# Split parts of x read in place as matmul weights, gathered windows placed by a table, b2 added after the last block

## The reference

```python
msg = node_feat[src] + edge_feat
neigh = jax.ops.segment_sum(msg, dst, num_segments=3125)
rst = (1.0 + eps[0]) * node_feat + neigh
h = rst @ W1 + b1                      # 128 -> 256
h = relu((h - mean(h, 0)) * rsqrt(var(h, 0) + 1e-5) * gamma + beta)
out = h @ W2 + b2                      # 256 -> 128
x = layernorm(x + out)                 # over the 128 features
```

## Time and profile before

| | |
|---|---|
| median of 3 runs | 280.7 us (280.33 to 281.25) |
| the profiled execution, its own time | 281.48 us |
| its span, first to last instruction | 279.7 us |
| mean granted TensorE clock | 0.964 of full speed |
| busy in the span | PE 244.9, DVE 208.4, POOL 181.2, ACT 131.7 us |

### The profile page before, as it was taken

One profiled execution on the slowest core, in us unless ns is written; L12 is line 12 of the kernel. 1 busy time (PEld: TensorE's weight loads), 2 busy tenths in 40 slices (PEclk: granted clock), 3 DMA queues, 4 the chain that ended last, 5 costly groups with the idle time before them and its releaser, 6 DMA issues.

```text
span 279.7 us, 7102 instructions
## 1 busy us (share of the span) xinstructions
PE 244.9 (88%) x2211; PEld 200.6 (72%) x2211; DVE 208.4 (75%) x916; ACT 131.7 (47%) x236; POOL 181.2 (65%) x117
## 2 busy tenths in 40 slices
PE   1567989999998889988899999999999859999970
PEld 1456768899987677766788888777878648844870
DVE  3888997788998778778489887876867861178990
ACT  0327864455555535545255544444443302086494
POOL 2078888888888888888888888888888920000000
PEclk9999999999999999999599999999999968999995
DMA  5955766687888777788488888776665200000033
GB/s 165 285 172 108 147 145 137 156 191 197 189 195 185 178 164 171 181 179 183 96 172 192 174 195 171 167 179 145 150 126 105 53 2 0 2 0 1 2 114 116
DMA packets 49535, 38.39 MB, mean 137 GB/s; under 512 B 5083, under 2 KB 48523, under 8 KB 49497
## 3 DMA queue, kind: packets, MB, share of 16 engines
q1 hardware_dynamic: 32829, 30.62, 38.2%
q0 software_dynamic: 14976, 6.82, 20.4%
q10 hardware_dynamic: 1692, 0.48, 0.9%
HBM read 36.31 MB, written 1.60 MB: 136 GB/s over the span
## 4 chain that ended last, share of the span: by engine, by line
PE 46%; DMA 16%; issue 14%; POOL 9%; DVE 7%; ACT 4%; SPq 2%; DVEq 0%; ACTq 0%; POOLq 0%
PE ps L641 18%; PE ps L649 12%; DMA egat<-in_x_dram,srci 9%; POOL egat L402 9%; DMA egat<-in_edge_attr_dram 7%; PE ps L679 5%; PE ps L673 4%; PE ps L595 4%; ACT big L527 3%; PE ps L665 2%; SPq L321 1%; DVE big L1033 1%; DVE big L1035 1%; PE ps L670 1%; DVE hit_l L904 1%
## 5 line engine op out<-in xcount | busy, mean ns | idle before, releaser
L402 POOL DMA_INDIRECT egat<-in_x_dram,srci x104 | 172.2, 1656 | 44.0 <-issue 29.2
L488 ACT ACTIVATE big<-ps 128x500 f32 x156 | 95.1, 610 | 119.8 <-PE ps L679 91.6
L641 PE MATMUL ps<-big,xp 128*128 128x114 f16 (+8 forms) x675 | 116.9, 280 | 0.2 <-issue 0.2
L649 PEld LDWEIGHTS ps<-hit_c,ebuf 128*128 128x128 f32 x624 | 101.8, 194 | 16.6 <-DVE aggT L983 6.1
L649 PE MATMUL ps<-hit_c,ebuf 128*128 128x20 f32 x624 | 95.1, 230 | 9.1 <-DVE aggT L983 5.0
L641 PEld LDWEIGHTS ps<-big,xp 128*128 128x128 bf16 x675 | 63.0, 110 | 14.6 <-issue 1.1
L983 DVE TENSOR_TENSOR aggT<-aggT,ps 128x20 f32 x208 | 35.8, 172 | 49.8 <-PE ps L649 39.7
L910 DVE TENSOR_TENSOR hit_k<-iota_k,key 128x400 f16<-128x400 f16 x156 | 56.1, 359 | 0.0
L904 DVE TENSOR_TENSOR hit_l<-iota_k,lo 128x256 f16<-128x256 f16 x156 | 52.1, 334 | 1.7 <-issue 1.6
L679 PE MATMUL ps<-hit_k,hit_l 128*128 128x400 f16 x156 | 52.3, 335 | 0.0
L908 DVE TENSOR_TENSOR hit_k<-iota_k,key 128x300 f16<-128x300 f16 x156 | 48.2, 309 | 0.0
(11 more groups left out here) (101 smaller groups left out, 165.5 us busy)
## 6 DMA issues: line engine op xcount, KB each, us to landing
ebuf<-in_edge_attr_dram SPq DMA_DIRECT2D x78, 256.0 KB
egat<-in_edge_attr_dram SPq DMA_DIRECT2D x51, 128.0 KB
egat<-in_x_dram,srci POOLq DMA_INDIRECT x104
out_dram<-big SPq DMA_DIRECT2D x6, 256.0 KB
w_sb<-in_L_gnn_W_dram ACTq DMA_DIRECT2D x2, 128.0 KB, 6.8
rows<-in_dst_dram SPq DMA_DIRECT2D x1, 192.0 KB
rows<-in_src_dram ACTq DMA_DIRECT2D x1, 192.0 KB
egat<-in_edge_attr_dram SPq DMA_DIRECT2D x1, 66.0 KB
```

The costliest lines, as they stand in the source:

```text
L402: return nc.gpsimd.indirect_dma_start(to, None, x[:, :], bass.IndirectOffsetOnAxis(ap=ix, axis=0), compute_op=op)
L488: nc.scalar.activation(cnt[:, :, bass.ds(lows[m % LOADS], WIN)], ps[:, m % BANKS_C, 0:KEYS].rearrange("p (t n) -> p t n", n=WIN), ACT.Copy ...
L641: last = nc.tensor.matmul(ps[:, ACC + f % 2, 0:SIZES[f]], xp[:, t, n, :], cnt[:, t, STARTS[f]:STARTS[f] + SIZES[f]], start=(u == 0), stop= ...
L649: last = nc.tensor.matmul(ps[:, SUMS + w % BANKS_S, 0:WIN], rows_v[:, j * D:(j + 1) * D], hits_v, start=(j == 0), stop=(j == ROWS - 1))
```

## The change

Three edits:

1. `xp` goes. `xr` gets room for all 25 tiles, part 2 gets a tensor of its own (`x3`), and the matmuls of parts 0 and 1 take as weights the upper halves of the fp32 words of `xN` and `xr` directly, that is every second bf16. ACT's fourteen copies and their semaphores go, and so do the waits of `rest` on them.
2. Which windows are gathered is decided by `arrange`, in the program's construction: it adds up costs in cycles window by window, and makes a window gathered when the running sum reaches GATHER_FIRST + n * GATHER. The last window stays gathered.
3. As b2's addition changes `xN`, which is now read by the matmuls, POOL waits with it for the last block's matmuls.

```diff
+ROUNDS = 12
+SUM = 670
+COUNT = 770
+KEPT = 810
+HITS = 2400
+TURN = 1680
+GAP = 14
+GATHER = 9360
+GATHER_FIRST = 10200
...
-    def in_window(w):
-        return (w + 1) * NG // G > w * NG // G
-
-    C_AT = [w for w in range(G) if not in_window(w)]
-    G_AT = [w for w in range(G) if in_window(w)]
+    def spans(c_at):
+
+        return [c_at[g - 1] + SETTLE for g in ENDS[:-1]] + [G]
+
+    def share(ready, w):
+
+        for f in range(F - 1):
+            if ready[f] <= w < ready[f + 1]:
+                n, i = ready[f + 1] - ready[f], w - ready[f]
+                return f, UNITS * i // n, UNITS * (i + 1) // n
+        return 0, 0, 0
+
+    def arrange():
+
+        order = [(w + 1) * NG // G > w * NG // G for w in range(G)]
+        for _ in range(ROUNDS):
+            ready = spans([w for w in range(G) if not order[w]])
+            now, m, n, order = 0, 0, 0, []
+            for w in range(G):
+                gathered = n < NG - 1 and w < G - 1 and (m == GC or now >= GATHER_FIRST + n * GATHER)
+                gathered = gathered or w == G - 1
+                f, u0, u1 = share(ready, w)
+                own = SUM if gathered else max(SUM + COUNT + KEPT * (m < KEEP), HITS)
+                now += own + (u1 - u0) * (SIZES[f] + GAP) + TURN * (X_RATE * w < NT)
+                order.append(gathered)
+                m, n = m + (not gathered), n + gathered
+            short = NG - sum(order)
+            at = [w for w in range(G) if not order[w]]
+            for w in at[len(at) - short:] if short > 0 else []:
+                order[w] = True
+        return order
+
+    IN_WINDOW = arrange()
+    C_AT = [w for w in range(G) if not IN_WINDOW[w]]
+    G_AT = [w for w in range(G) if IN_WINDOW[w]]
...
-        xp = sb("xp", [P, NT, PARTS, D], BF16)
+        xr = sb("xr", [P, NT, D])
+        x3 = sb("x3", [P, NT, D], BF16)
...
                 pool.wait_ge(x_rest_made, NB)
-                pool.wait_ge(x_first_made, NB)
+                pool.wait_ge(block_multiplied, F)
...
-                    if m % SPREAD == SPREAD // 2 - 1 and m // SPREAD < NB:
-                        b = m // SPREAD
-                        t0, t1 = pieces(b)
-                        nc.scalar.activation(xp[:, t0:t1, 0, :], upper(xN[:, t0:t1, :]), ACT.Copy).then_inc(x_first_made, 1)
-                        act.wait_ge(x_rest_made, b + 1)
-                        nc.scalar.activation(xp[:, t0:t1, 1, :], upper(xr[:, b % 2, 0:t1 - t0, :]),
-                                             ACT.Copy).then_inc(x_middle_made, 1)
...
                         if f == 0 and u % (4 * PARTS) == 0:
-                            pe.wait_ge(x_first_made, t // 4 + 1)
-                            pe.wait_ge(x_middle_made, t // 4 + 1)
+                            pe.wait_ge(x_rest_made, t // 4 + 1)
                             pe.wait_ge(x_last_made, t // 4 + 1)
...
-                        last = nc.tensor.matmul(ps[:, ACC + f % 2, 0:SIZES[f]], xp[:, t, n, :],
+                        part_v = x3[:, t, :] if n == 2 else upper((xN, xr)[n][:, t:t + 1, :])[:, 0, :]
+                        last = nc.tensor.matmul(ps[:, ACC + f % 2, 0:SIZES[f]], part_v,
...
-                    if b >= 2:
-                        dve.wait_ge(x_middle_made, b - 1)
-                        dve.wait_ge(x_last_made, b - 1)
```

More of the change, by code:

```diff
@@ L82, in gnn_layer @@
     KEYS = NT * WIN
-    def in_window(w):
-        return (w + 1) * NG // G > w * NG // G
-    C_AT = [w for w in range(G) if not in_window(w)]
-    G_AT = [w for w in range(G) if in_window(w)]
+    UNITS = NT * PARTS
+    def spans(c_at):
[27 more added lines that the diff above has]
+    G_AT = [w for w in range(G) if IN_WINDOW[w]]
     C_OF = {w: m for m, w in enumerate(C_AT)}
     G_OF = {w: n for n, w in enumerate(G_AT)}
-    READY = [C_AT[g - 1] + SETTLE for g in ENDS[:-1]] + [G]
-    UNITS = NT * PARTS
+    READY = spans(C_AT)
     def units(w):
[L95 to L99, removed]
+        return share(READY, w)
     EARLY = STARTS[-1] // BANK
@@ L167, in gnn_layer @@
         srcq = rows[0:Q, 1, 0:QW].bitcast(I32)
-        xr = rows[:, :, 0:QW].rearrange("p a (t d) -> p a t d", d=D)
         firsts = sb("firsts", [1, G], I32)
@@ L236, in gnn_layer @@
         x_rest_made = sem("x_rest_made")
-        x_first_made = sem("x_first_made")
-        x_middle_made = sem("x_middle_made")
         x_last_made = sem("x_last_made")
@@ L927, in rest @@
                     t0, t1 = pieces(b)
-                    if b >= 2:
-                        dve.wait_ge(x_middle_made, b - 1)
-                        dve.wait_ge(x_last_made, b - 1)
-                    nc.vector.tensor_tensor(xr[:, b % 2, 0:t1 - t0, :], xN[:, t0:t1, :], upper(xN[:, t0:t1, :]),
+                    nc.vector.tensor_tensor(xr[:, t0:t1, :], xN[:, t0:t1, :], upper(xN[:, t0:t1, :]),
                                             ALU.subtract).then_inc(x_rest_made, 1)
@@ L936, in part_3 @@
                     t0, t1 = pieces(b)
-                    v = xr[:, b % 2, 0:t1 - t0, :]
+                    v = xr[:, t0:t1, :]
                     dve.wait_ge(x_rest_made, b + 1)
-                    nc.vector.tensor_tensor(xp[:, t0:t1, 2, :], v, upper(v), ALU.subtract).then_inc(x_last_made, 1)
+                    nc.vector.tensor_tensor(x3[:, t0:t1, :], v, upper(v), ALU.subtract).then_inc(x_last_made, 1)
                 def add_block(f, done):
```

## The result

297.27 us (297.02 to 299.5, four runs) against 280.51 us: a ratio of 1.064, 95% interval 1.057 to 1.072. The prediction was 299.1 us, with 292 to 305 as its range.

The account below looks back on a forecast made before the run. Bound: gathers at GpSimd's own pace, with group 50 at window 181. Landing at 218.1 us plus 43.7 of work gives 261.8; 36.27 behind gives span 298.1, plus 1.8 is 299.9, less 0.8 is 299.1 us; range 292 to 305.

Parts of the forecast that it names:

- GpSimd as an independent clock, 3.87 us a group: GpSimd's gather queue: runs by itself at 3.87 us per group of two gathers; no part of the kernel makes it late.
- Window 181 at 218.1 us: PE at group 50's gathered window, moved from 203 to 181: can start only when the gather lands, 218.1 us.
- my 4.5 us: Gather landing: a row is there for PE some 4.5 us after its group's second gather starts, seen 3.78 to 5.44.
- The work behind it, 43.7 us: PE from window 181 to the last multiply: 43.7 us of work, ending at 261.8 instead of 243.43, +18.4 us.
- The table's charge too high, since it adds what overlaps: `arrange`, counted windows: multiplies added on top of 2400 cycles give 1.66 us where the trace has 1.18; gathers placed too early.
- b2 added late: GpSimd's b2 addition moved behind the last multiply: removes PE's 3.72 us stall and 3.4 us of half clock, -7.1 us.
- Stepped loads, 0 to +1.7: PE's 450 loads of parts 0 and 1 reading every second bf16: taken as 0, at most +1.7 us in blocks 7 and 8.
- the 5.9 us without it: Stepped loads in the end without the fast load: 107 ns a load, 100 x 59 ns = 5.9 us.
- ScalarE 8 us less: ScalarE: fourteen copies go, 4.0 us for part 0 and as much for part 1, so it is busy 8 us less.
- GpSimd's addition beside the bn_stats, 0 to +4.5: b2's addition at its new place: DVE not held, taken as 0; at most +4.5 us if bn_stats are held.
- the number and length of the waits for gathers: PE's waits for gathers: 35 to 45 us in about forty waits instead of 7.9 us in nine.
- before window 181 the waits absorb them: Falls of PE's clock before window 181: 3.4 us each, absorbed by waits; one near 218 us costs 3.4 in full.

Follow-up runs that it names:

- the table alone: The kernel before with only the change's constants, `spans`, `share` and `arrange`; parts of x still copied, b2 added early: 302.2 us, ratio 1.086.
- the even order: The changed kernel with the table replaced by the old rule, gathered windows again every fourth: 273.8 us, ratio 0.983 to the kernel before.
- the two doses: The changed kernel with GATHER = 10400 instead of 9360 (group 50 at window 193): 284.7 us; with 9900 (window 187): 289.7 us.
- the kernel with half the gathers: The changed kernel with the second gather of each group left out and PE waiting for one alone: 264.3 us, ratio 0.949 to the kernel before.
- mending the charge alone: The changed kernel with arrange charging a counted window the larger of DVE's 2400 cycles and PE's work including multiplies: 267.02 us, ratio 0.954 to the kernel before.
- the two measured kernels: The changed kernel with gathered windows again every fourth, 273.8 us; the kernel before with only b2 added after the last block's multiply, 274.8 us.

## Why the prediction was right, step by step

- **GpSimd as an independent clock, 3.87 us a group:** shown, and less exact than two decimals say. It is 3.84 us in the changed kernel and 3.78 with the table alone ((209.49 - 24.03) / 49). In the eleven profiled executions with all gathers the last one starts between 213.35 (the table alone) and 217.31 (the kernel before), which doesn't follow the order of the windows: the even order has 214.44.
- **Window 181 at 218.1 us:** 217.78. The count of additions, 181 by 218.3 us, is the forecast's own number. That it came within 0.3 us is partly luck: in the profiled execution the second gather of group 50 started 1.4 us earlier than before (212.20 for 213.57), and PE, slowed by the last fall of the clock, came 1.1 us after the 216.7 at which my 4.5 us have it land. With the table alone the window starts at 213.43. That the position of group 50 carries the loss is shown by the two doses and by the kernel with half the gathers.
- **The work behind it, 43.7 us:** 43.6, in the changed kernel and in the one with half the gathers. The profiled execution took 299.5 us where 299.9 was forecast; its median lies 2.2 us below that, where I had taken 0.8.
- **The table's charge too high, since it adds what overlaps:** shown by mending the charge alone, 297.3 to 267.0 us.
- **b2 added late:** the mechanism stands. In the even order there is no DVE instruction of 7.9 us, and the addition runs inside the hidden layer's stretch. The size was off in the even order: -7.1 was forecast, -4.8 and -3.8 us were measured against medians of the same chip. The term was taken from one profiled execution, at 281.48 us slower than every other run of that kernel. Its mean granted clock was 0.964; in the runs beside the two measured kernels it was 0.975 to 0.986, as in those two themselves (0.971 to 0.987). So it seems that the fall of the clock, 3.4 us of the term, is mostly missing there and the wait of 3.72 us is what was gained; no trace of such a run shows it. In the changed kernel the term shows as a dense end without a stall. With the table alone, where the stall is in that end, the profile has the term in full, 6.9 us; the medians have 4.9 (302.2 for 297.3), or 7 if each is taken by its ratio to the kernel before of its own rounds.
- **Stepped loads, 0 to +1.7:** 0. The mean of a load is 109 to 111 ns for the stepped and the plain ones of the changed kernel alike, and block 8 takes 3.63 us as before, 48 ns for a load and its matmul. The Trainium skill (TensorE: Matmul & The Clock Gate, "Weight-path perf modes") says that the fast load takes strided columns; the trace agrees for a step of two, and the 5.9 us without it did not come.
- **ScalarE 8 us less:** 6.0 (131.7 to 125.7). The two kinds of copies take 4.0 us each, but their records overlap their neighbours', and a busy time is the union. It changes nothing in the sum.
- **GpSimd's addition beside the bn_stats, 0 to +4.5:** 0. GpSimd and DVE in the changed kernel:

```profile
261.40 0.27 DVE L970 TENSOR_TENSOR aggT<-aggT,ps 128x110 f32<-128x110 f32 x1 [2.78 <-PE ps L668]
261.76 6.98 POOL L463 TENSOR_TENSOR xN<-xN,b2e 128x3200 f32<-128x3200 f32 x1 [44.31 <-PE ps L668]
...
264.76 0.69 DVE L1037 BATCH_NORM_STATS2 big<-big 128x6 f32<-128x512 f32 x1 [0.16 <-ACT big L532]
```

  The bn_stats keep their 0.69 us (mean of the fourteen 624 ns, as before), and GpSimd needs 6.98 us instead of 7.55. This is the rule of the Trainium skill (SBUF — State Buffer, "Who interferes with whom") with both of its sides: one SBUF input isn't held, two are, and only by a GpSimd instruction that reads.
- **What failed:** the number and length of the waits for gathers. The step "before window 181 the waits absorb them" was right, and the count of 35 to 45 us didn't follow it through: a fall of the clock doesn't only use up waits, it removes them from the list. An estimate closes most of the gap: 20.8 us of waits, the some 12 us that the low clock took, and the some 5 us by which the terms are short over these windows, as the kernel with half the gathers shows, make 38. For the result it made no difference but the last fall's 1 us.

## What to carry to other kernels

When one engine consumes in a fixed order what another makes at a pace of its own, the position of the last item matters, not the mean rate: the end is that item's arrival plus all the work placed behind it, and both can be read from the trace of before. A cost table for such an order has to charge the larger of two overlapping engines, not their sum; here the sum put the items up to 22 positions earlier than an even spacing (up to 25 earlier than the mended table) and cost 23 us, and the larger of the two gained some 7 us over the even spacing. A few us of bookkeeping on GpSimd that read SBUF are best placed where DVE runs instructions with one SBUF input.

## What the runs showed of the hardware that was not expected

The GpSimd addition of b2, beside which a DVE comparison waits, takes 7.55 us, and the same one beside bn_stats 6.98 us; it was 7.55 in both kernels in which DVE was held and 6.98 or 6.99 in the ten others. And idle time of PE can go unseen: in the changed kernel PE is busy 85% of the span, but it ran four stretches like the one at 203.4 us at 1.2 GHz, busy 6.70 of 6.70 us there, in a stage that waits for gathers. Busy shares have to be read beside the granted clock.
